# Four basis buffers and four staging rows in the graph kernel's build stage, with its constants, loads and waits in another order

## The reference, cut to what matters

```python
w = jnp.einsum('rb,bio->rio', att, basis)      # att (2, 30), basis (30, 512, 512), twice
...
msgs.append(gate[:, None] * x_j @ w[r])
...
agg = jax.ops.segment_sum(msg, row, num_segments=x.shape[0])
```

## Time and profile before

| | us |
|---|---|
| median of 3 runs | 2070.17 (2068.27 to 2072.72) |
| the profiled execution, device time | 2070.58 |
| its span (first to last instruction) | 2068.6 |
| mean granted TensorE clock | 0.969 of full |

### The profile page before, as it was taken

How to read it: one execution, slowest core, us unless ns; L and a number is a source line. 1 busy time by engine, 2 the same in 40 slices (tenths; PEclk the granted TensorE clock), 3 DMA queues, 4 the chain that set the end, 5 groups by cost and what they waited for, 6 DMA issues and landing times.

```text
span 2068.6 us, 23800 instructions
## 1 busy us (share of the span) xinstructions
PE 1900.6 (92%) x7966; PEld 907.6 (44%) x7978; DVE 799.5 (39%) x1978; ACT 626.5 (30%) x1200; POOL 7.8 (0%) x27
## 2 busy tenths in 40 slices
PE   4878888589999989999999999999999999987998
PEld 2545554353333434444444444444444445433443
DVE  5666677424111162110111223354444544384122
ACT  1544544414666042111211000132232323275100
POOL 1000000000000000000000000000000000000000
PEclk9999999879999969999999999999999999998999
DMA  5889889670100052100000010700000000021011
GB/s 119 219 204 228 218 202 224 180 274 0 36 1 1 0 173 102 41 0 1 1 21 31 31 41 31 307 29 5 21 6 21 6 21 1 16 66 56 21 51 41
DMA packets 47379, 157.54 MB, mean 76 GB/s; under 512 B 9316, under 2 KB 11260, under 8 KB 38816
## 3 DMA queue, kind: packets, MB, share of 16 engines
q1 hardware_dynamic: 42880, 142.28, 23.9%
q10 hardware_dynamic: 4384, 13.78, 1.9%
HBM read 120.38 MB, written 35.65 MB: 75 GB/s over the span
## 4 chain that ended last, share of the span: by engine, by line
PE 78%; DMA 7%; DVE 5%; ACT 4%; issue 2%; DVEq 1%; another core or an unknown queue 1%; SPq 0%; POOL 0%; ACTq 0%; POOLq 0%
PE psum L1195 29%; PE psum L1181 28%; PE psum L1413 6%; DMA hs<-in_L_gnn_basis 6%; PE psum L1264 3%; PE psum L1098 2%; PE psum L1317 2%; PE psum L1364 2%; PE psum L1130 2%; PE psum L1129 1%; ACT adj L878 1%; DMA hs<-in_x 1%; DVE hs L582 1%; DVE hs L584 1%
## 5 line engine op out<-in xcount | busy, mean ns | idle before, releaser
L1195 PE MATMUL psum<-hs,adj 128*128 128x512 f16 x2880 | 643.0, 380 | 0.8 <-DVE hs L689 0.8
L1181 PE MATMUL psum<-wb,xt 128*128 128x512 f32 x1152 | 511.6, 602 | 15.5 <-DVE hs L817 13.4
L1195 PEld LDWEIGHTS psum<-hs,adj 128*128 128x128 f16 x2880 | 280.1, 98 | 354.0 <-issue 37.1
L1181 PEld LDWEIGHTS psum<-wb,xt 128*128 128x128 f32 x1152 | 219.2, 193 | 286.0 <-issue 283.9
L970 ACT ACTIVATE adj<-hs,pbias 128x512 f32<-128x512 f32 x216 | 134.5, 708 | 86.1 <-PE psum L1264 86.1
L1130 PE MATMUL psum<-hs 128*128 128x192 f32 x636 | 159.2, 333 | 0.0
L1003 ACT ACTIVATE ua<-ua 128x512 f32<-128x512 f32 x60 | 37.9, 631 | 335.3 <-DVE ua L831 187.6
L582 DVE TENSOR_SCALAR hs<-hs 128x128 f32<-128x128 f16 x318 | 89.8, 282 | 105.7 <-PE psum L1130 63.1
L1413 PE MATMUL psum<-hs,adj 128*128 128x512 f32 x288 | 123.8, 592 | 0.0
L768 DVE TENSOR_TENSOR vt<-psum,adj 128x512 f32<-128x512 f32 x24 | 16.6, 692 | 271.9 <-PE psum L1181 271.9
L1130 PEld LDWEIGHTS psum<-hs 128*128 128x128 f32 x636 | 117.0, 197 | 7.2 <-issue 1.2
(11 more groups left out here) (213 smaller groups left out, 1478.8 us busy)
## 6 DMA issues: line engine op xcount, KB each, us to landing
hs<-in_L_gnn_basis SPq DMA_DIRECT2D x64, 960.0 KB, 8.2
aw_scratch<-xt ACTq DMA_DIRECT2D x12, 768.0 KB, 5.5
adj<-aw_scratch SPq DMA_DIRECT2D x1, 9216.0 KB, 38.1
x_scratch<-adj SPq DMA_DIRECT2D x24, 256.0 KB, 2.2
hs<-x_scratch SPq DMA_DIRECT2D x24, 256.0 KB, 2.6
ts_scratch<-adj SPq DMA_DIRECT2D x1, 4608.0 KB, 17.9
as_scratch<-adj SPq DMA_DIRECT2D x1, 4608.0 KB, 30.1
adj<-ts_scratch SPq DMA_DIRECT2D x1, 4608.0 KB, 14.5
```

The lines of the kernel that those rows point to most:

```text
L1181: x = pe.matmul(psum[:, bank, :], xt[:, i, k, :], w[:, k, :], start=first and k == 0, stop=last and k == 3)
L1195: x = pe.matmul(psum[:, i % 2 + (4 * half if own else 0), :], adj[:, m, j, P * i:P * i + P], hs[:, t, half, j, :], start=n == 1 or (own an ...
```

## The change

- Two further chunk buffers lie in the last three rows of `adj` planes 1 and 2, which the turn lots of blocks 9 to 11 write; so chunks 0 to 51 rotate over four buffers and chunks 52 to 63 over the first two. Chunk n goes to buffer (n + 1) % 4, so that the buffer over the edges is chunk 3's. Chunks 0 to 2 are loaded straight behind the edges, chunk 3 where chunk 0 was loaded before. Each buffer's next chunk is loaded when PE has used its last.
- Four staging rows (`mixed`: the two of `ua`, and two in a spare part of `wb`) instead of two.
- The 16 `att` loads are issued by ACT as its first instructions instead of by SP. `attw` is formed ahead of the wait for `wrow_ps`.
- POOL makes the identity, then the small iotas, `attw`'s zeros and the window iota, then the rest. DVE starts on the edges alone and waits for five constants at L509, PE starts on two.
- The drains and `built` are gone. SP loads x groups 0 to 2 when PE has done the first of the last six turn lots, `Wf` when it has done them all, and the saves of `adj` wait for ACT's last copy. DVE waits for the last `row_out` ahead of x tile 6, and for the small loads behind the copy of the image features.

```diff
...
         onehot_w = lay(STEP * AWW, F32, "p (k c) -> p k c", k=STEP)
         basis = [flat[:, 0:4 * D * 2].bitcast(F32), lay(4 * D, F32)]
+        for m in (1, 2):
+            basis.append(adj[:, m, NT - 3:NT, :].rearrange("p j n -> p (j n)")[:, 0:4 * D * 2].bitcast(F32))
+        FAR_CHUNKS = 52
+        def basis_of(n):
+            return (n + 1) % 4 if n < FAR_CHUNKS else (n + 1) % 2
+        def nth_of(n):
+            return len([m for m in range(n + 1) if basis_of(m) == basis_of(n)])
+        def follower(n):
+            return min([m for m in range(n + 1, 64) if basis_of(m) == basis_of(n)], default=None)
         aw_stage = xt[:, :, :, :].rearrange("p a b d -> p (a b d)")[:, 0:2 * NT * P].rearrange("p (k j d) -> p k j d", k=2, j=NT)
...
+        spare = wb[:, :, :, :].rearrange("p a b n -> p (a b n)")[:, 2 * NT * P:2 * NT * P + 2 * D].rearrange("p (k n) -> p k n", k=2)
+        mixed = [ua[:, 0, :], ua[:, 1, :], spare[:, 0, :], spare[:, 1, :]]
         typed = wb[:, :, :, :].rearrange("p a b n -> p (a b n)").bitcast(F16)[:, 0:2 * 2 * NT * P].rearrange("p (k m j d) -> p k m j d", k=2, m=2, j=NT)
...
-        built = sem("built")
...
-        basis_in = [sem(f"basis_in{k}") for k in range(2)]
-        comb_out = [sem(f"comb_out{k}") for k in range(2)]
+        basis_in = [sem(f"basis_in{k}") for k in range(4)]
+        comb_out = [sem(f"comb_out{k}") for k in range(4)]
...
             for a, name in enumerate(("src", "dst", "edge_type_2")):
                 sp.dma_start(erow_i[0:ER, a, :], ins[name].rearrange("(r e) -> r e", e=256)).then_inc(edges_in, 16)
             sp.dma_start(erow[0:ER, 3, :], ins["edge_weight"].rearrange("(r e) -> r e", e=256)).then_inc(edges_in, 16)
-            for l in range(2):
-                for t in range(2):
-                    for j in range(4):
-                        sp.dma_start(attc[j:120:4, l, t:t + 1], ins[f"L1_gnn_att{l + 1}"][t].unsqueeze(1),
-                                     allow_slow_non_contiguous=True).then_inc(weights["att"], 16)
             def load_chunk(n):
                 l, c = n // (CH // 2), n % (CH // 2)
-                sp.dma_start(basis[n % 2][0:120, :], bases[l][:, c * (4 * D):(c + 1) * (4 * D)]).then_inc(basis_in[n % 2], 16)
+                sp.dma_start(basis[basis_of(n)][0:120, :], bases[l][:, c * (4 * D):(c + 1) * (4 * D)]).then_inc(basis_in[basis_of(n)], 16)
+            for n in range(3):
+                load_chunk(n)
             sp.wait_ge(ecol_ps, 1)
             sp.wait_ge(span_ready, 4)
-            load_chunk(0)
-            load_chunk(1)
+            load_chunk(3)
             for n in range(CH):
                 l, c = n // (CH // 2), n % (CH // 2)
                 lot = lot_of[("basis", l, c)]
-                if n + 2 < CH:
+                if follower(n):
                     sp.wait_ge(side_ps, lot + 1)
-                    load_chunk(n + 2)
+                    load_chunk(follower(n))
                 sp.wait_ge(side_out, side_copied(lot))
                 for q in range(4):
-                    sp.dma_start(combs[l][q, :, c, :], ua[32 * q:32 * q + 8, n % 2, :]).then_inc(comb_out[n % 2], 16)
-            sp.wait_ge(row_out, 16 * (NT + 1))
-            sp.wait_ge(built, 4)
+                    sp.dma_start(combs[l][q, :, c, :], mixed[n % 4][32 * q:32 * q + 8, :]).then_inc(comb_out[n % 4], 16)
+            sp.wait_ge(side_ps, len(side) - 5)
             def x_tile(src, i):
                 return src[P * i:P * i + P, :]
...
             x3 = ins["x"].rearrange("(g k p) d -> g p k d", p=P, k=3)
             for g in range(NT // 3):
                 if g == 3:
+                    sp.wait_ge(side_ps, len(side))
+                    sp.wait_ge(typed_summed, BLOCKS)
                     sp.dma_start(wf, ins["L0_gnn_Wf"].rearrange("(k p) n -> p k n", p=P)).then_inc(weights["wf"], 16)
                     sp.wait_ge(x_ps, 3 * (g - 2))
                     sp.wait_ge(x_sq, 3 * (g - 2))
...
+            sp.wait_ge(side_out, side_copied(len(side) - 1))
             sp.dma_start(ts_dram, adj_flat[2]).then_inc(weights["ts_out"], 16)
             sp.dma_start(as_dram, adj_flat[0]).then_inc(weights["as_out"], 16)
...
             def first_of_l1():
-                for k in range(2):
-                    sp.wait_ge(comb_out[k], 64 * 33)
+                for k in range(4):
+                    sp.wait_ge(comb_out[k], 64 * 17)
                 sp.wait_ge(o_ps, tick(0, NT - 1))
                 sp.wait_ge(acc_ps, tick(0, NT - 1))
                 sp.wait_ge(g2_ps, 1)
...
             pool.affine_select(out=ident[:], in_=ident[:], compare_op=ALU.not_equal, fill=1.0, base=0,
                                pattern=[[-1, P]], channel_multiplier=1).then_inc(c_ready, 1)
             pool.wait_ge(c_ready, 2)
-            pool.tensor_copy(ident16[:], ident[:])
-            pool.memset(zeros, 0.0)
-            pool.memset(ones[:], 1.0)
-            pool.memset(gw[:], 0.0)
-            pool.memset(wa_pad[:], 0.0)
-            pool.memset(attw[:], 0.0)
-            pool.memset(bcol[:, 5:6], 1e-5).then_inc(c_ready, 1)
-            pool.iota(iota_s, [[1, REL * TW]], base=0, channel_multiplier=0,
-                      allow_small_or_imprecise_dtypes=True).then_inc(c_ready, 1)
             pool.iota(win16, [[W, NW]], base=0, channel_multiplier=0,
                       allow_small_or_imprecise_dtypes=True).then_inc(c_ready, 1)
...
                       allow_small_or_imprecise_dtypes=True).then_inc(c_ready, 1)
             pool.iota(tileno[:, 2:4], [[-1, 2]], base=int(FAR), channel_multiplier=-2,
                       allow_small_or_imprecise_dtypes=True).then_inc(c_ready, 1)
+            pool.memset(attw[:], 0.0).then_inc(c_ready, 1)
+            pool.iota(iota_s, [[1, REL * TW]], base=0, channel_multiplier=0,
+                      allow_small_or_imprecise_dtypes=True).then_inc(c_ready, 1)
+            pool.memset(zeros, 0.0)
+            pool.tensor_copy(ident16[:], ident[:])
+            pool.memset(ones[:], 1.0)
+            pool.memset(gw[:], 0.0)
+            pool.memset(wa_pad[:], 0.0)
+            pool.memset(bcol[:, 5:6], 1e-5).then_inc(c_ready, 1)
             for k in range(STEP):
                 pool.sem_inc(onehot_free[k], 1)
-            for k in range(2):
+            for k in range(4):
                 pool.sem_inc(comb_out[k], 64)
             for b in range(RING):
                 pool.sem_inc(win_free[b], 1)
...
                 x = pool.tensor_scalar(krel[:, 1, a, :], krel[:, 0, a, :], float(-by), None, ALU.add)
             x.then_inc(krel_ready, 1)
-            pool.drain().then_inc(built, 1)
             n_all = 0
             for r in [0, 2, 3, 4, 5, 6, 7, 8]:
...
                 ins_.then_inc(dve_done, 1)
                 dve.wait_ge(dve_done, n_dve[0])
-            dve.wait_ge(c_ready, 7)
             dve.wait_ge(edges_in, 64)
             dve.tensor_scalar(erow_i[0:ER, 3, :], erow_i[0:ER, 0, :], P - 1, None, ALU.bitwise_and)
             dve.tensor_copy(erow_d[0:ER, :], erow_i[0:ER, 1, :])
...
             dve.tensor_reduce(trange[0:ER, 0:2], dst2, AX.X, ALU.min)
             step(dve.tensor_reduce(trange[0:ER, 2:4], dst2, AX.X, ALU.max))
             step(dve.tensor_scalar(trange[0:ER, 0:2], trange[0:ER, 0:2], float(-W), None, ALU.add))
+            dve.wait_ge(c_ready, 5)
             for h in range(2):
                 dve.tensor_scalar(spant[0:ER, h, :], win16[0:ER, :], trange[0:ER, h:h + 1], None, ALU.is_gt)
             step(dve.tensor_copy(wcol[0:ER, 0:1], tileno[0:ER, 0:1]))
...
             step(dve.tensor_tensor(wcol[0:NW, 3:4], wcol[0:NW, 1:2], wcol[0:NW, 2:3], ALU.subtract))
             step(dve.tensor_scalar(wcol[0:NW, 3:4], wcol[0:NW, 3:4], 1.0, None, ALU.max))
             dve.tensor_scalar(wcol[0:NW, 3:4], wcol[0:NW, 3:4], 1.0 / STEP, 0.5 - 0.5 / STEP, ALU.mult, ALU.add).then_inc(wcol_ready, 1)
+            dve.wait_ge(c_ready, 6)
+            dve.wait_ge(weights["att"], 16 * 16)
+            step(dve.tensor_reduce(attm[0:120, :], ident[0:120, 0:120].rearrange("p (b j) -> p j b", j=4), AX.X, ALU.add))
+            for l in range(2):
+                for t in range(2):
+                    x = dve.tensor_scalar(attw[0:120, l, 4 * t:4 * t + 4], attm[0:120, :], attc[0:120, l, t:t + 1], None, ALU.mult)
+                x.then_inc(attw_ready, 1)
             dve.wait_ge(wrow_ps, 1)
             v = psum[0:1, 4, 0:2 * NW].rearrange("p (a w) -> p a w", a=2)
             step(dve.tensor_copy(wrow_i[0:1, 0:2, :], v))
...
             dve.tensor_tensor(wrow_i[0:1, 0, :], wrow_i[0:1, 0, :], wrow_i[0:1, 3, :], ALU.bitwise_or).then_inc(ranges_ready, 1)
             dve.wait_ge(ranges_ready, 1)
-            dve.wait_ge(weights["att"], 16 * 16)
-            step(dve.tensor_reduce(attm[0:120, :], ident[0:120, 0:120].rearrange("p (b j) -> p j b", j=4), AX.X, ALU.add))
-            for l in range(2):
-                for t in range(2):
```

(36 more changed lines are left out.)

## The result

The changed kernel takes 2041.82 us in the median of four runs (2040.93 to 2044.66) against 2071.44 for the kernel before beside it (2068.27 to 2073.64): a ratio of 0.986, with an interval of 0.984 to 0.988. The forecast was 2040.8 in a range of 2027 to 2053. The profiled execution took 2040.93 us, its span 2039.1.

A forecast was written before the change was run, and what follows sets the result against it. DVE and PE were taken to set the loop's pace in turn, PE stalling for chunks, with waits before and behind the loop. Gains of 4.3 + 13.5 + 11.6 = 29.4 us gave 2040.8 us from the median, range 2027 to 2053.

The forecast's parts named there:

- Start: Up to the first window: DVE begins on the edges alone, `att` lands at 18.3, first window at 24.1; gain 4.3 us.
- so 2.3 more: At the start: extra landing time of `att` beside chunk loads, from `aw_scratch` taking 5.5 us beside them and 3.23 alone.
- The bound: Lower end at the start: `att` lands a few us behind a third chunk, first window at 28, gain 0.
- The packet rule: Rival at the start: `att` passes between whole chunk packets, landing at 19.2; gain 3.4, total 2041.7; 0.70 together with the forecast.
- Loop: Window loop: four chunk buffers remove 23.6 us of PE's waits for chunks, of which 13.5 us reach the pace.
- 57%: Window loop: share of a PE stall that reaches the pace, 1.16 of 2.03 us in one stalled window.
- Staging rows at nothing: Window loop: ACT's 13.1 us of waits for staging rows counted at no gain, with up to 5 us as bound.
- Behind the loop: From the loop to `Wim`'s product: x asked for 8.0 us earlier, `Wi`'s product 12.9 earlier; gain 11.6 us.
- `Wim` now ends last: Ahead of `Wim`'s product: `Wim` lands at 442.0, 1.3 us after PE is ready at 440.7.
- The queues: Rival in the loop: DMA queues bound it, gain there 5 or so, total 21, 2049 us; chance 0.14.
- The rival of stalls at full length: In the loop: stalls count in full, with half clock behind long ones; loop gain 24 to 28, 2028 us; chance 0.12.
- The staging rival: In the loop: staging writes behind up to four chunk loads land late; kernel over 2070, say 2078 us; chance 0.04.

The follow-up runs named there:

- all chunks were late: The changed kernel with chunks 0 to 3 all loaded behind ecol_ps and span_ready, as chunk 0 was before: 2038.19 us, ratio 0.981 to the kernel before.

## Why the forecast held, by its own steps

**Start: wrong sign.** The step that failed is "so 2.3 more", the price of small loads beside chunks. I had taken it from `aw_scratch`, 768 KB in large pieces, and it came out at over 10: `att` was there at 26.5, not 18.3, and DVE stood at that wait beyond 20, the sign that the prediction had named. The bound was wrong too. It had `att` a few us behind a third chunk and no gain at worst; `att` did come 4.0 us behind the third chunk, but that chunk landed at 22.5, where 19.2 was taken. Chunk 3, asked for at 14.83, was under way as well. Edges at 8.85 instead of 6 were the same error and cost nothing further, since the `att` wait hid them. The last stretch, from the weights to the first tile, took 0.6 us more than 4.7, in the gap ahead of that tile (2.75 against 2.11 in the earlier trace rows). POOL's idle time ahead of the identity was 8.74 us against 9.36 before; over all fourteen profiles it was 8.45 to 10.44, with no sign of the traffic in it (8.72 where all chunks were late).

**The packet rule** was the rival nearer the truth. The Trainium skill (DMA: Bandwidth & Descriptors, Queues, rings and completion order) has each engine drain a whole packet of one queue before it turns to the next. The runs agree in direction: the same four small loads took 3.9 us alone and 15.2 beside chunks. They don't show the packets themselves. My use of it, three chunks and then `att` at 19.2, was still too mild by 7 us: 3.3 for the third chunk, and 4.0 behind it.

**Loop: right mechanism, mis-sized.** The waits that went were those foretold (27.6 to 3.6, the rest behind chunk 52). The share that reaches the pace was not 57%: 24.0 us of PE's waits returned 20.4, or 85%. Less what can be clock (3.4) it is 71% at least, so the share alone lies between the two. I had read it from one window. DVE's own account says much the same: its waits for PE fell by 25.2, and its gaps of loop overhead, now no longer hidden in them, grew from 42.2 to 48.8, so 18.6 net. One stalled window was too few for such a share. Staging rows at nothing: right, and shown.

**Behind the loop: right within 1.3 us, by another path.** That x is asked for 8 us earlier and that the image features no longer wait for small loads are each borne out by undoing them, 6.8 us (2.0 of it `Wim`'s landing) and 5.7. Together that is more than 10.3; both act on when `Wi`'s product starts, so they can't be added. "`Wim` now ends last" was wrong: it landed at 389.6 + 35.7 = 425.3, and PE came at 427.2, so PE's own work sets the end there. PE came later than forecast because `Wi` took 12.1 us where "about 10" was taken: its product gained 11.1 us, not 12.9, and from there to `Wim`'s product PE took 36.2 us, not 35.5. The forecast had 12.9 for PE and took 11.6 because of `Wim`; so its number lies nearer to the 10.3 than its reason does.

**The rivals.** The queues do not bound the loop: a share of 0.89 at a higher rate. The rival of stalls at full length, with half clock behind long ones, had 24 to 28 us in the loop; the 20.4 lie about midway between it and the 13.5, and its half clock is in the trace. The staging rival, the one on the slower side, is refuted: with half the rows ScalarE waited 42.8 us and nothing followed. (Its own sum is off by 2: at 0.75 us for each of 52 chunks, less 29.4, the kernel would end at 2080, not 2078.)

## What to carry to other kernels

In this kernel a tiny load that others wait for had to land before the bulk loads started, and to be asked for first was not enough; holding 2.9 MB of prefetch back for 5 us was worth 10 us. Before a cheap transfer is moved out of a queue, look at what it keeps back: in this kernel nine small loads had, by all that the timeline shows, been shielding a 1 MB load from 9 MB of saves. And a forecast that comes out right in sum should be opened into its stretches before its reasons are believed.

## What had not been expected of the hardware

- Loads of 480 bytes took 15.2 us to land beside 960 KB loads on another queue and 3.9 without them.
- `Wi` on ScalarE's queue took 12.1 us beside x and small loads, and 35.2 when two 4.6 MB saves on SyncE's queue began 2.9 us behind it.
- One load of 120 bytes, issued 0.11 us behind the first chunk, took 9.1 us to land; the 15 ahead of it took 2.1 us in the median.
- With one start and one code, the wait for `att` ended anywhere from 22.8 to 27.9 us; the loop behind it kept within 335.6 to 338.1 in all eleven profiles with four buffers.
- In the kernel before, PE's granted clock was at half for 3.4 us behind each of three waits for a chunk (1.76 to 3.14 us), and the 3.3 us by which the stretch behind `Wim` differs between the two kernels goes with 89 us at half clock against 79.
